# A graph attention layer on one core: where TensorE's items and VectorE's scans stand in a batch's slot

## The reference

```python
x = x + _L0_gnn_ref(_layernorm(x), edge_index, L0_gnn_W, L0_gnn_b)
x = x + _L0_ffn_ref(...)
x = x + _L1_gnn_ref(_layernorm(x), edge_index, L1_gnn_W, L1_gnn_a_src, L1_gnn_a_dst)
x = x + _L1_ffn_ref(...)

def _L1_gnn_ref(x, edge_index, W, a_src, a_dst):        # 8 heads of 32 columns
    x_proj = (x @ W).reshape(n, H, D)
    alpha_src = jnp.einsum('nhd,hd->nh', x_proj, a_src)
    alpha_dst = jnp.einsum('nhd,hd->nh', x_proj, a_dst)
    row, col = (edge_index[0], edge_index[1])
    e = alpha_src[row] + alpha_dst[col]
    m = jax.ops.segment_max(e, col, num_segments=n)
    m = jnp.where(jnp.isfinite(m), m, 0.0)
    e_exp = jnp.exp(e - m[col])
    s = jax.ops.segment_sum(e_exp, col, num_segments=n)
    att = e_exp / (s[col] + 1e-16)
    out = jax.ops.segment_sum(att[:, :, None] * x_proj[row], col, num_segments=n)
    return out.reshape(n, H * D)
```

## Time and profile before

| | |
|---|---|
| median of 3 runs | 3641.34 us (3639.1 to 3643.8) |
| the profiled execution: its time | 3640.77 us |
| its span in the profile | 3639.0 us |
| the slots of this stage | 2121.8 us (first subtraction) to 3184 us |
| busy over the span | PE 76%, DVE 50%, ACT 31%, POOL 47% |

### The profile page before, as it was taken

How to read it: one execution, slowest core, us unless ns; L and a number is a source line. 1 busy time by engine, 2 the same in 40 slices (tenths; PEclk the granted TensorE clock), 3 DMA queues, 4 the chain that set the end, 5 groups by cost and what they waited for, 6 DMA issues and landing times. The chain is left out here.

```text
span 3639.0 us, 56893 instructions
## 1 busy us (share of the span) xinstructions
PE 2782.9 (76%) x13194; PEld 2293.0 (63%) x13195; DVE 1826.4 (50%) x4258; ACT 1131.4 (31%) x4199; POOL 1722.6 (47%) x1811
## 2 busy tenths in 40 slices
PE   1477788888875899999996727777667777638999
PEld 0356666666653788888885525555555555538998
DVE  5324454454457111111112758888788878773444
ACT  0001110000011222222221435555555555524444
POOL 0677777777770232222222077777777777200000
PEclk9988888898887899999998858888888888857999
DMA  5333333333330222222222544333333333100000
GB/s 175 92 105 110 110 112 112 110 110 109 110 108 19 81 85 83 84 87 83 86 85 63 180 110 109 106 106 106 106 106 104 107 106 105 41 18 10 20 20 20
DMA packets 152212, 327.43 MB, mean 90 GB/s; under 512 B 38743, under 2 KB 89905, under 8 KB 147938
## 3 DMA queue, kind: packets, MB, share of 16 engines
q0 software_dynamic: 85824, 236.38, 23.1%
q1 hardware_dynamic: 59762, 83.04, 6.9%
q10 hardware_dynamic: 6480, 6.42, 0.5%
HBM read 286.42 MB, written 41.40 MB: 90 GB/s over the span
## 5 line engine op out<-in xcount | busy, mean ns | idle before, releaser
L633 POOL DMA_INDIRECT G<-g_rows,srcT x784 | 744.8, 950 | 393.5 <-issue 237.7
L633 POOL DMA_INDIRECT G<-h_rows,srcT x784 | 753.7, 961 | 252.0 <-issue 237.8
L817 PE MATMUL pS<-G,O 128*128 x2336 | 568.6, 407 | 144.7 <-SPq L804 106.7
L1728 PE MATMUL pS<-G,O 128*128 x2336 | 625.6, 430 | 43.2 <-DVE O L1876 32.6
L817 PEld LDWEIGHTS pS<-G,O 128*128 128x128 f32 x2336 | 475.8, 205 | 233.9 <-issue 155.7
L1728 PEld LDWEIGHTS pS<-G,O 128*128 128x128 f32 x2336 | 483.3, 210 | 180.3 <-issue 68.5
L1793 ACT ACTIVATE G<-G 128x32 f32<-128x32 f32 x2352 | 503.2, 307 | 0.0
L1386 ACT ACTIVATE HE<-pH,b1s 128x256 f32<-128x256 f32 x432 | 204.9, 474 | 583.4 <-PE pH L1361 583.4
L1361 PE MATMUL pH<-XT,w1s 128*128 128x256 f32 x1728 | 383.8, 380 | 1.4 <-SPq L1332 1.4
L1371 PE MATMUL pY<-w2s,HE 128*128 128x256 f32 x1728 | 381.9, 379 | 0.0
L1361 PEld LDWEIGHTS pH<-XT,w1s 128*128 128x128 f32 x1728 | 329.6, 191 | 46.9 <-issue 1.8
(11 more groups left out here) (301 smaller groups left out, 3391.2 us busy)
## 6 DMA issues: line engine op xcount, KB each, us to landing
w1s<-in_W_dram SPq DMA_DIRECT2D x16, 1024.0 KB, 5.2
w2s<-in_W_dram SPq DMA_DIRECT2D x16, 1024.0 KB, 7.8
G<-h_rows,srcT POOLq DMA_INDIRECT x784, 2.8
Y<-y_rows SPq DMA_DIRECT2D x49, 256.0 KB, 4.4
G<-g_rows,srcT POOLq DMA_INDIRECT x784, 2.8
g_rows<-OUT SPq DMA_DIRECT2D x49, 132.0 KB, 2.4
h_rows<-ACC SPq DMA_DIRECT2D x7, 896.0 KB, 5.5
X<-in_x_dram SPq DMA_DIRECT2D x1, 6144.0 KB
```

The costliest lines, as they stand in the source:

```text
L633: pool.indirect_dma_start(out=G[:, c % (ring * Q), 0:width], out_offset=None, in_=rows, in_offset=bass.IndirectOffsetOnAxis(ap=srcT[:, c:c ...
L817: mm = nc.tensor.matmul(pS[k][:, 0:W], O[:, k, q, :], G[:, bass.ds((s % R0) * Q + q, 1), :].rearrange("p a d -> p (a d)"), start=(q == 0), ...
L1728: mm = nc.tensor.matmul(pS[:, bass.ds((w % BANKS) * BANK, NR)], O[:, k, q, :], G[:, bass.ds((s % R) * Q + q, 1), 0:NR].rearrange("p a d -> ...
```

## The change

In TensorE's slot the call of `turn_scores(b + 1)` goes from ahead of the items of batch b-1 to behind them. In VectorE's slot the items of b-1 go ahead of the scans of b+1; the two bounds of `span`, which were read under the first scan, are read ahead of the items. Nothing is added or taken away: each engine has as many instructions as before.

```diff
                             tr.then_inc(s_mt, 1)
-                            if ahead:
-                                turn_scores(b + 1, k + 1)
                             pe.sem_inc(s_seen, 1)
                             if before:
                                 items(pairs_before, b - 1)
+                            if ahead:
+                                turn_scores(b + 1, k + 1)
...
                             dve.sem_inc(s_prep, 1)
                             loc.restart()
-                            pairs_of = (lambda: span(dve, b - 1)) if before else (lambda: None)
-                            pairs_before = scans(b + 1, pairs_of) if ahead else pairs_of()
                             if before:
-                                items(pairs_before)
+                                items(span(dve, b - 1))
+                            if ahead:
+                                scans(b + 1)
```

## The result

| | before | changed |
|---|---|---|
| median | 3641.02 us (3639.1 to 3643.8, 4 runs) | 3817.86 us (3815.11 to 3819.36, 4 runs) |
| profiled execution: time, span | 3640.77, 3639.0 | 3815.11, 3813.4 |
| slots 2 to 47 | 979.2 | 1154.3 |
| mean slot with one pair, with two | 17.11, 25.47 | 21.14, 29.05 |

The changed kernel takes 1.0484 times as long (95% interval 1.0466 to 1.0502), 176.8 us more, where 156.4 was forecast. The span grew by 174.4, and all of it lies in the stage: slots 2 to 47 took 175.1 more, slot 1 3.3 more (29.27 against 25.97), while the time up to slot 1 was 2.2 us and the time behind the last subtraction 1.9 us shorter. The place is as forecast, and so is the manner in the main: busy times are nearly as before, in a longer stage. What sets L1858's place in the slot is not as forecast, and that is what the experiments were for.

The account below looks back on a forecast made before the run. VectorE's own program was taken to set the pace. Slots 2 to 47 would take 153.1 us more and slot 1 3.3, together 156.4 on 3640.77: 3797 us, range 3765 to 3840.

Parts of the forecast that it names:

- What bounds the kernel before: VectorE's own program sets the pace: 17.00 us a slot with one pair of items, 24.91 with two.
- Step 1: VectorE reads the bounds ahead of the items: 0.92 us added, mattering only if the wait for `fac` does not swallow it.
- Step 2: `fac` stands behind ScalarE's 48 scalings, at 11.63 after the subtraction, putting L1858 at 11.99: 1.55 us a slot.
- Steps 3 and 4: After L1858, 2.54 and 0.35 us as before, then 5.78 from scans to subtraction, with 1.20 of uncovered trip to TensorE.
- Step 5: TensorE's pair, 7.64 us or 9.59 after idling, costs nothing up to 10.5; second blocks may start as late as 10.6.
- In return VectorE's waits for TensorE go: In slots 2 to 47, the better part of 15.3 us of VectorE's old waits would vanish.
- The prediction's own sign of being wrong: In the profile after, L1876 waiting for TensorE in most slots would show that the clock sets the pace.
- The faster one: TensorE's wait ahead of the scores' transposes was the hidden bound: 15.3 us less, 3625 us; chance 0.03.
- The one without a wait for `fac`: ScalarE's scalings would not delay L1858, which stands at 10.44: 73 us fall away, 3724 us; chance 0.04.
- The clock: TensorE stays at half clock through each slot's first pair, 15.3 us: 4.7 more a slot, 4018 us; chance 0.04.

Follow-up runs that it names:

- e8: The kernel before, with 10 extra matmuls in TensorE's idle time between the turned maxima and the scores' transposes: 3646.07 us, ratio 1.0015.
- e10: The kernel before, with ScalarE scaling 7 of the 16 chunks instead of 6: 3626.90 us, ratio 0.9963.
- e7: The changed kernel, with the bounds of a batch's items read under the first scan of the slot before: 3813.75 us, ratio 1.0483.
- e2: The changed kernel, with ScalarE doing its part of the items between the first and second half of its 48 scalings: 3819.04 us, ratio 1.0481.
- e1: The changed kernel with TensorE's scores' transposes back ahead of the items, leaving only VectorE's half of the change: 3814.07 us, ratio 1.0471.
- e3: The changed kernel, with 16 extra matmuls a slot on TensorE behind the scores' transposes: 3804.65 us, ratio 1.0445.
- e5: The changed kernel, with 18 extra matmuls behind the scores' transposes and 2 between the maxima's transposes and the items: 3796.48 us, ratio 1.0427.

## Why the prediction was right, and where it was not

The direction, the place and most of the size were right: 156 us forecast, 177 measured, in the range.

*What bounds the kernel before.* Right. e8 shows it from one side (a warmer TensorE gives nothing), e10 from the other (0.27 us off VectorE's slot gives 13 us).

*Step 1, the bounds.* Right that they would be swallowed; in e7, where they are read early, no gain is resolved.

*Step 2, fac.* The moment was right: 11.64 after the subtraction in the slot shown, forecast 11.63, and in 44 of the 46 slots right behind the scalings. As a cause it was half of the truth. "So L1858 is at 11.99 in every slot" failed; it stood at 12.40 in the mean and waited for `fac` for 4.4 us in all instead of 65 to 70.

*Steps 3 and 4, the rest of the pair and the trip.* Right: 8.78 us in the mean from L1858 to the next subtraction in slots with one pair, forecast 8.67, with a trip of 1.20 us in each slot, 54.0 in 45. Slot 1 took the 3.3 us more that were forecast.

*Step 5, TensorE, costed at nothing.* This term was mis-sized. It allowed a pair 10.5 us and held 9.59 to be the worst. Two numbers were too small. The items start 0.72 us after the maxima's transposes, not 0.13: in slot 48 of the earlier trace rows TensorE had come straight from other items, whereas now it waits for the maxima just before, and its loads and branch into the loop are bare. And after 9 us of idle time ahead of the transposes the pair takes up to 10.66. So the second blocks stood at up to 11.89, and past the limit of 10.7 in 27 of 46 slots. That puts L1858 0.41 us a slot later, 19 of the 22 us that the forecast missed in slots 2 to 47 (175.1 against 153.1); the other 3 lie between L1858 and the next subtraction. It was named as what would push the time up, with the limit at the right place, but thought of as an exception; it sets more than half of the slots. "In return VectorE's waits for TensorE go" failed with it: the blocks' waits for TensorE went from 31.7 us to 216.0. The prediction's own sign of being wrong, that L1876 waits for TensorE in most slots, came true: the second blocks waited for it in all 46. That the total came within 21 us in spite of this is in part luck. With `fac` early (e2) TensorE alone still puts L1858 at 12.20 in the mean, so the term put at nothing was about as large as the one for `fac`, and the two nearly coincide instead of adding up.

*The rivals.* The faster one fell: TensorE's 248.8 us of idle time bounded nothing. In e1 they are gone and the kernel is slower; in e8 they are partly filled and nothing is gained. The Trainium skill ("Perfetto Trace Analysis", Optimization Strategies) gives high utilization of the matmul engine as the general goal, and when it idles, to optimize the engines that block the critical path. The goal alone would have led astray here; its words on the critical path are what has to be checked first. The one without a wait for `fac` fell in e2, though for another reason than I gave: the wait was there, but doubled. The clock was a true mechanism of a much smaller size, up to 3 us on a pair (10.66 against 7.64) and not 7.6, and most of that lay under `fac`.

## What to carry to other kernels

Before moving work so that an engine's longest idle time goes, ask whether anybody waits for that engine; here nobody did, and the move laid bare three things that the old order had covered: a round trip to another engine, another engine's long loop, and that engine's slow start. When two engines become late at nearly the same moment the profile names the later one alone, and taking either away gives almost nothing; price both from their own rows, and take both away in one run. A row from the end of a stage is a good model for a new order, but look at what its engines had been doing just before.

## What the runs showed of the hardware that I had not expected

The granted clock can fall after dense work has begun. In e3 TensorE idled 2.36 and 1.15 us around a 0.64 us piece, and the clock fell as the items began. In 19 of the 46 slots it fell only behind their start, by up to 1.42 us. In the slot where it was latest the gaps were 1.59 and 1.05 us and the items began at 2971.73 (columns as in the earlier trace rows):

```profile
2972.50:2973.00 0.50, 0.50 (x4) 0.40 (x3) 0.50 (x1) 0.50 (x3) 0.00 (x0) 1.00 0.16 66
2973.50:2974.00 0.50, 0.50 (x2) 0.38 (x2) 0.50 (x1) 0.50 (x4) 0.00 (x0) 0.50 0.00 0
```

So gaps that are only nearly closed may bring little. The 16 extra matmuls a slot of e3 raised the clock in the stage from 0.77 to 0.91 and bought 13 us, by the shorter trip alone, with L1858 where it was. The 18 and 2 of e5, at a clock of 0.95, bought 21, and left 24 of the 46 first pairs partly cold.
